# A Mamba and mixture-of-experts layer on one core: steps of the first block, of the norm and of the hand-over to the experts in another order

## The reference

```
x = L0_attn_x                                   # [4, 1024, 256]
# Mamba: D_STATE = 16, D_CONV = 4, D_INNER = 512
xp, res = split(x @ W_in.T)
xc = silu(causal_depthwise_conv(xp, conv_w) + conv_b)
B, C, dt = split(xc @ W_x.T);  dt = softplus(dt @ W_dt.T + b_dt);  A = -exp(A_log)
h = exp(A * dt_t) * h + dt_t * B_t * x_t        # a scan over the tokens, for 16 states
y = silu(sum over states of h * C_t + D * x_t + res) @ W_out.T
x = layernorm(x + y)
# mixture of experts: 8 experts, the best 2 for each token
p = softmax(x @ router_w.T);  w, idx = top_k(p, 2);  w = w / (sum(w) + 1e-9)
out = sum over the 2 of w * (gelu(x @ w1[e].T + b1[e]) @ w2[e].T + b2[e])
x = layernorm(x + out)
```

## Time and profile before

| what | us |
|---|---|
| runs: median (lowest to highest) | 1448.56 (1444.14 to 1448.6) |
| profiled execution: time | 1448.68 |
| its span in the trace | 1447.1 |
| PE busy in the span | 1292.0 |
| VectorE busy | 1099.3 |
| GpSimd busy | 1062.2 |
| ScalarE busy | 994.6 |

### The profile page before, as it was taken

The page is one execution under the profiler, slowest core; times in us unless marked ns, Lnnn a source line. Parts: engine busy times, 40 slices in busy tenths (PEclk is TensorE's granted clock), DMA queues, the critical chain, the costliest instruction groups (busy, mean ns, idle before and its releaser), DMA issues. The chain is left out here.

```text
span 1447.1 us, 28836 instructions
## 1 busy us (share of the span) xinstructions
PE 1292.0 (89%) x8807; PEld 1097.5 (76%) x8808; DVE 1099.3 (76%) x1830; ACT 994.6 (69%) x1366; POOL 1062.2 (73%) x925
## 2 busy tenths in 40 slices
PE   5599899999999998998997997299999999999990
PEld 2367777787787787777886886299999999999980
DVE  5678989988999898899898893666565665665654
ACT  6699998997998998999988962333433434334334
POOL 4379888798998989988989997445555555555545
PEclk8799999999999999999999997599999999999996
DMA  8423222132232232332322336423564732622216
GB/s 272 153 71 102 71 93 95 48 118 81 81 118 77 75 121 75 99 103 74 100 88 70 109 94 228 131 58 61 153 173 108 211 69 46 166 39 40 37 20 240
DMA packets 91019, 150.76 MB, mean 104 GB/s; under 512 B 10893, under 2 KB 43277, under 8 KB 90929
## 3 DMA queue, kind: packets, MB, share of 16 engines
q1 hardware_dynamic: 73216, 121.24, 26.0%
q0 software_dynamic: 16704, 27.29, 9.7%
q10 hardware_dynamic: 1008, 1.07, 0.2%
HBM read 100.79 MB, written 48.78 MB: 103 GB/s over the span
## 5 line engine op out<-in xcount | busy, mean ns | idle before, releaser
L1425 POOL TENSOR_TENSOR arena<-arena 128x1024 f32<-128x1024 f32 x256 | 607.3, 2387 | 17.7 <-DVE arena L1105 11.5
L490 PE MATMUL d_ps<-ident,arena 128*128 128x128 f32 x2048 | 320.9, 280 | 37.1 <-DVE arena L1105 30.9
L490 PEld LDWEIGHTS d_ps<-ident,arena 128*128 128x128 f32 x2048 | 244.2, 144 | 139.0 <-DVE arena L1105 61.1
L1105 DVE TENSOR_TENSOR_SCAN arena<-arena,d_ps 128x512 f32<-128x512 f32 x256 | 302.0, 1207 | 45.6 <-PE d_ps L490 35.1
L1105 DVE TENSOR_TENSOR_SCAN arena<-arena,carry,d_ps 128x512 f32<-128x512 f32 x256 | 314.6, 1264 | 23.0 <-PE d_ps L490 16.0
L793 ACT ACTIVATE arena<-u_tok,b_tok 128x512 f32<-128x512 f32 x508 | 324.5, 712 | 6.0 <-PE d_ps L490 5.1
L503 PE MATMUL y_ps<-ident,arena 128*128 128x128 f32 x2048 | 300.0, 276 | 7.6 <-POOL arena L1425 6.9
L1772 ACT ACTIVATE h_t<-ht_ps 128x512 f32<-128x512 f32 x142 | 84.4, 594 | 289.0 <-PE ht_ps L1827 289.0
L807 ACT ACTIVATE arena<-dt,neg_a 128x2048 f32<-128x2048 f32 x127 | 253.3, 1994 | 2.1 <-DVE arena L1105 1.9
L503 PEld LDWEIGHTS y_ps<-ident,arena 128*128 128x128 f32 x2048 | 240.5, 143 | 10.4 <-POOL arena L1425 8.5
L1812 PE MATMUL h_ps<-arena,xg_t 128*128 x852 | 218.3, 405 | 0.6 <-issue 0.6
(11 more groups left out here) (230 smaller groups left out, 1556.2 us busy)
## 6 DMA issues: line engine op xcount, KB each, us to landing
arena<-c_rows SPq DMA_DIRECT2D x128, 256.0 KB, 3.3
arena<-weight_parts SPq DMA_DIRECT2D x20, 1024.0 KB, 5.6
weight_parts<-arena SPq DMA_DIRECT2D x64, 256.0 KB, 3.6
xg<-expert_rows POOLq DMA_DIRECT2D x71, 130.0 KB, 2.4
arena<-in_pieces SPq DMA_DIRECT2D x16, 512.0 KB, 8.4
arena<-in_pieces SPq DMA_DIRECT2D x64, 128.0 KB, 3.4
expert_out<-arena SPq DMA_DIRECT2D x1, 4224.0 KB, 15.3
weight_parts<-arena SPq DMA_DIRECT2D x4, 1024.0 KB, 4.5
```

Of the source, the lines that this page charges most:

```text
L490: last = nc.tensor.matmul(d_ps[:, c % 2, j * P:(j + 1) * P], ub[:, g % U_RING, j, c * P:(c + 1) * P], t.ident[:], start=True, stop=True, i ...
L1105: nc.vector.tensor_tensor_scan(h[:, g % H_RING, c, :], decay[:, g % D_RING, c, :], d_ps[:, c % 2, :], 0.0 if i % 2 == 0 else carry[:, n, c ...
L1425: nc.gpsimd.tensor_tensor(h[:, g % H_RING, lo:hi, :], h[:, g % H_RING, lo:hi, :], c_row[:, g % C_RING:g % C_RING + 1, :].broadcast_to([P, ...
```

## The change

At the **start**, the two instructions that split `sizes` go from ScalarE and GpSimd to VectorE, ahead of `low_size`. ScalarE's `first_part(2)` goes ahead of `silu_chunk(3)`. The reads of chunk 0 and chunk 1 of block 1 go ahead of and behind the second half of the first decay, and wait for one half of dt instead of two. `halo_fix` of block 1 goes ahead of the second product of step 1. The silu call of block 1 is written apart.

At each **block boundary**, `variance` goes from (12, 2) to (11, 1) and `rstds` from step 12 to step 11, as they stood in iteration 7 already. `normed` goes from step 13 to step 14, except in iteration 7, which keeps step 12. Since its call stands behind those of `scale` and `decays` of a step while the copies stand ahead of them, it passes three copies, a scaling and a decay.

In the **tail**, the four products of steps 126 and 127 go from GpSimd to VectorE (`last_products`), behind the last scan. The first sends of block 5 go from steps 13 and 15 of iteration 7 into `end`. The routers' steps, the weight splits, the sends and the `ranks` matmuls stand in another order, and ScalarE's table loads are written out. In `experts`, the second turn of x goes behind the first up-projection.

```diff
@@ mamba: PE, end() @@
-                    for k in range(4 * STATE - 2):
+                    for k in range(4 * STATE):
                         if SUM_AT[k] >= 4 * STATE:
                             sum_states(r, k)
-                    ranks()
-                    for k in range(4 * STATE - 2, 4 * STATE):
-                        sum_states(r, k)
                     turn_group(0)
                     turn_group(1)
+                    ranks()
                     out_group(0)
@@ ScalarE @@
-                            act.wait_ge(dt_done, 2)
+                            act.wait_ge(dt_done, 1)
...
                 def end():
-                    router_exp()
+                    nc.scalar.preload_act_table_set("silu_and_others")
                     for j in range(TT):
                         y_silu_group(j)
-                    nc.scalar.activation(var[:, TT:TT + 1], t.ones[:, 0:1], ACT.Exp)
-                    own_high(0)
-                    own_high(1)
+                    nc.scalar.preload_act_table_set("natural_log_exp_and_others")
+                    router_exp()
+                    for m in range(4):
+                        own_high(m)
                     copy_rows(0)
                     copy_rows(1)
-                    own_high(2)
                     copy_rows(2)
                     copy_rows(3)
+                    own_high(4)
+                    own_high(5)
                     router_exp(r)
-                    for m in range(3, 2 * W_LOADS):
-                        own_high(m)
+                    own_high(6)
+                    own_high(7)
...
                     first_part(1)
-                    act.wait_ge(sizes_raw, 32)
-                    nc.scalar.copy(y_u[0:Z_ROWS, 1].bitcast(F32R), y_u[0:Z_ROWS, 0]).then_inc(sizes_high, 1)
+                    first_part(2)
                     silu_chunk(3)
...
                     first_ssm_out()
-                    first_part(2)
                     first_part(3)
...
                     first_decay(0)
+                    xp_out(e, 0)
                     first_decay(1)
-                    xp_out(e, 0)
+                    xp_out(e, 1)
...
                     decays(1)
-                    xp_out(e, 1)
...
-                    if back and n == (12 if i == BLOCKS - 1 else 13):
+                    if back and n == (12 if i == BLOCKS - 1 else 14):
                         normed()
@@ VectorE @@
+                def last_products():
+                    dve.wait_ge(hc_done, 2 * (STEPS - LAST_PRODUCTS))
+                    for g in range(STEPS - LAST_PRODUCTS, STEPS):
+                        dve.wait_ge(c_loaded[g % C_RING], 16 * (g // C_RING) + 16)
+                        for lo in (0, 2):
+                            dve.wait_ge(scan_done, 4 * g + lo + 2)
+                            nc.vector.tensor_tensor(h[:, g % H_RING, lo:lo + 2, :], h[:, g % H_RING, lo:lo + 2, :],
+                                                    c_row[:, g % C_RING:g % C_RING + 1, :].broadcast_to([P, 2, T]),
+                                                    ALU.mult).then_inc(hc_done, 1)
                 def end():
+                    last_products()
                     router_pick()
+                    copy_group(0)
+                    copy_group(1)
+                    router_sum()
+                    router_invert()
                     router_rank()
-                    router_sum()
-                    copy_group(0)
-                    router_invert()
-                    copy_group(1)
                     router_place()
+                    own_low(0)
                     copy_group(2)
...
-                    own_low(0)
                     own_low(1)
+                    own_low(2)
                     router_pick(r)
-                    router_rank(r)
+                    own_low(3)
+                    own_low(4)
                     router_sum(r)
                     router_invert(r)
+                    router_rank(r)
                     router_place(r)
...
+                    dve.wait_ge(sizes_raw, 32)
+                    nc.vector.tensor_copy(y_u[0:Z_ROWS, 1].bitcast(F32R), y_u[0:Z_ROWS, 0]).then_inc(sizes_high, 1)
+                    dve.wait_ge(sizes_high, 1)
+                    nc.vector.tensor_tensor(t.sizes[:].bitcast(F32R), y_u[0:Z_ROWS, 2], y_u[0:Z_ROWS, 1],
+                                            ALU.subtract).then_inc(sizes_split, 1)
                     low_size()
...
-                            if at == ((11, 1) if i == BLOCKS - 1 else (12, 2)):
+                            if at == (11, 1):
                                 variance()
@@ GpSimd @@
             def times_c(g, half):
                 b, n = divmod(g, STATE)
+                if g >= STEPS - LAST_PRODUCTS:
+                    return
...
                 def end():
+                    for m in range(4):
+                        send_rows(BLOCKS - 3, m)
                     router_member()
                     router_shift()
-                    times_c(STEPS - 1, 1)
+                    send_rows(BLOCKS - 3, 4)
+                    send_rows(BLOCKS - 3, 5)
                     router_den()
...
+                    send_rows(p, 0)
+                    for j in range(TT):
+                        rstd_group(j)
+                        send_rows(p, j + 1)
...
+                    if i == 0 and n == 2:
+                        halo_fix(f)
                     if 0 <= g - 1 < STEPS:
                         times_c(g - 1, 1)
-                    if front and f % 2 == 1 and n == (2 if f == 1 else 1):
+                    if front and f % 2 == 1 and f > 1 and n == 1:
                         halo_fix(f)
...
-                    if back and n == (11 if i == BLOCKS - 1 else 12):
+                    if back and n == 11:
                         rstds()
-                    if place:
+                    if place and i < BLOCKS - 1:
@@ experts: PE (VectorE's x_rest(1, 1) goes behind bias_h(0) likewise) @@
             turn_x(0, 0)
-            turn_x(1, 1)
             e = expert_of(0)
             e_next = up(0, 0, e, after=1)
+            turn_x(1, 1)
```

27 lines of the change are left out of this document (11 added, 16 removed).

## The result

The changed kernel takes 1430.26 us (median of 4 runs, 1429.47 to 1431.87), the kernel before 1447.16 beside it (4 runs, 1444.14 to 1448.6): a ratio of 0.9885, 95% interval 0.9873 to 0.9897. The forecast was 1430.0. The profiled execution took 1429.47, with a span of 1427.7 against 1447.1. The prediction took 1448.56 for the median before; the median of those four runs is 1447.16. The medians are thus 16.9 us apart and the two profiled executions 19.2, since the profiled one before (1448.68) is slower than each of the four, and the profiled one after is the fastest of its four.

A forecast was written before the change was run, and what follows sets the result against it. PE is near full except at the start, around 870 to 930 us and at the end, where engines stand idle. Terms -11.0 + 2.7 - 9.4 - 1.0 = -18.7 from 1448.68 give 1430.0 us, range 1421 to 1439.

The forecast's parts named there:

- The three places: Where the prediction read each engine's timeline: the start (0 to 100 us), the block boundaries, and 850 to 950 us.
- Start, -11.0: Start: an earlier chunk 1 read and halo fix bring block 1's silu 11 us forward; bounds 8 to 12.
- The term for the scans: Start: the fourth scan begins at 47.8 instead of 56.60; 8.7 of the 11 us counted for the scans.
- the stretch behind it: Start, after those scans: the halo fix goes ahead of a 2.35 us product, counted as 2.3 us.
- Boundaries, +2.7: Block boundaries: blocks 1, 3, 5 lose 6.1 together, 2 and 4 gain 3.4, 6 nothing; bounds -3.4 to +8.
- The first rival: Boundaries: ScalarE has 2 us of slack in odd blocks, so the +6.1 goes and the time is 1424; 16%.
- Tail, -9.4: Tail: four products on VectorE, silu 8.1 earlier, last place at 901.0 instead of 910.44; bounds -7 to -10.5.
- Experts, -1.0: Experts: PE skips the second turn before the first up-projection, 1.3 earlier, of which 0.3 is returned.
- The third rival: Tail: VectorE's two-input products contend with GpSimd, the four cost 12.9 instead of 4.7, time 1438; 6%.
- the "against": Tail, argument against contention: GpSimd has only sends then, and two subtractions at 1.18 each had sends beside them.
- The second: Start: something other than the tap holds the early scans, so it gives 4 instead of 11, time 1437; 10%.
- fourth rivals: Boundaries: the norm's new place opens PE gaps and its clock falls; slower than before, 1457 at 5 us each; 2%.

The follow-up runs named there:

- e3: Changed kernel with the halo fix of block 1 put back behind the second product of step 1: 1433.61 us, ratio 0.9899.
- e5: Changed kernel with all four last products back on GpSimd, ahead of the first sends of block 5: 1433.46 us, ratio 0.9904.
- e6: Changed kernel with two of the four last products on VectorE and those of step 126 back on GpSimd: 1427.77 us, ratio 0.9868.
- e7: Changed kernel with the second turn of x ahead of the first up-projection again: 1429.68 us, ratio 0.9879.
- e4: Changed kernel with ScalarE's read of chunk 1 of block 1 back behind the decay of step 1: 1437.01 us, ratio 0.9924.

## Why the prediction was right, point by point

**What bounds the kernel.** The three places were the right ones, though the earlier trace rows has PE at 5 tenths in the first two slices only and at 9 in the next two. The last slots were not looked at, since the change leaves them alone; it does not, it moves them in VectorE's program.

**Start, -11.0; measured -12.3.** The mechanism held at each step: first scan 40.37 (forecast near 41), fourth scan after the tap at 46.50, halo fix 58.77 (59.4). The term for the scans was 0.6 short (the tap's read ended 0.6 earlier than worked out, since ScalarE's chain gained 1.3 and not 0.65 from the sizes), the stretch behind it 0.6: the lead grew by 2.9 there for a forecast 2.3, of which the fix is 2.1 by e3, and 0.8 come without it from a place that I did not find. It lies 0.3 outside the stated bounds of 8 to 12.

**Boundaries, +2.7; measured +0.8.** Signs and places were right in every block: odd -1.6, -1.7, -1.4, even +2.2 twice, block 6 -0.5 (from -1.0 to +0.7 in e5, e6 and e7). The term that was mis-sized is the one of each block: in block 1 the tap's wait grew from 0.20 to 2.04, by 1.84 and not by 2.0 (ScalarE had some 0.1 to spare ahead of the read), and 0.27 came back at step 13, since line 1162's collision is shorter where the statistics stand earlier (3.23 before, 2.96 in block 1). The even blocks gave 2.2 for 1.7, the 0.27 among it. The first rival ("the boundaries gain", because ScalarE has slack) was wrong: there was none.

**Tail, -9.4; measured -9.6.** The steps came as listed: products 4.61 (4.7), the silu 8.2 nearer (8.1), group 2's copy 7.3 (6.9), the last rung of GpSimd's ladder 7.7 (7.3), member 8.9 (9.1). What the prediction gave as the cause of the silu's gain, four products on VectorE, is 1.5 of it; the rest is that no sends stand ahead of products any more. It had both in its text, and put the price on the wrong one.

**Experts, -1.0; measured -1.1, of which e7 gives 0.7 to the edit.**

**The third rival,** VectorE against GpSimd, did not decide the tail: only sends lay beside the products, as the "against" said. Two of GpSimd's sends took 1.47 and 1.97 us beside them instead of 0.96, but GpSimd then waited 2.38 for VectorE anyway. The mechanism itself was real, and at work in two places where I had not priced it: the start (2.0 in the subtraction, 0.3 to 2.1 in the cast, whose end stands 0.28 behind GpSimd's) and line 1162.

**The second and fourth rivals** did not show: e4 is what the second would have looked like, and no gap of PE appeared at the norm.

**The sum** met the time because +3.2 and -2.8 nearly cancel, and because the forecast starts from 1448.68: against the medians it has 18.7 for 16.9. That it lies within 0.3 us of the measured 1430.26 is luck. Without the loss in the last slots it would have been 3 us too high, still inside its range.

## What to carry to other kernels

A step that waits between two others on a busy engine has two cures, to feed it earlier or to move it; do the first alone before both, since the wait of the engine's own neighbours may have been covering the step exactly (here the norm fits in ScalarE's 2.2 us wait for PE: early statistics alone bring 12.6 us, about half of them by fewer collisions, both together cost 1). Compare two traces by the lead at each step of the program, not by totals: it shows at once which stretch pays and which gives back. And when VectorE instructions of one form differ by a factor of two and more, lay GpSimd's timeline beside them before moving anything.
